# Sparse attention in an audio tower: the choice of places made per half of the batches, inside the work around it

## The reference, cut to what matters

```python
# L = 166: u = int(5 * ln(167)) = 25 places; 38 samples; H = 8 heads of D = 16
K_sample = K[:, :, idx_sample, :]
QK_sample = jnp.einsum('bhld,bhsd->bhls', Q, K_sample) * scale
M = QK_sample.max(axis=-1) - QK_sample.mean(axis=-1)
_, top_idx = jax.lax.top_k(M, u)                     # 25 of 166 places per batch and head
Q_reduce = jnp.take_along_axis(Q, top_idx[..., None], axis=2)
scores = jnp.einsum('bhud,bhld->bhul', Q_reduce, K) * scale
attn = jax.nn.softmax(scores, axis=-1)
V_top = jnp.einsum('bhul,bhld->bhud', attn, V)
out = jnp.broadcast_to(V.mean(axis=2, keepdims=True), (B, H, L, D))
out = out.at[b_idx, h_idx, top_idx].set(V_top)
```

## Time and profile before

| | |
|---|---|
| median of 3 runs | 2203.01 us (2197.26 to 2203.51) |
| profiled execution, its own time | 2204.3 us |
| its span | 2202.5 us |
| sampling | about 544 to 671 us |
| choice | about 671 to 682 us |
| second part of the attention | about 683 to 852 us |

### The profile page before, as it was taken

The page is one execution under the profiler, slowest core; times in us unless marked ns, Lnnn a source line. Parts: engine busy times, 40 slices in busy tenths (PEclk is TensorE's granted clock), DMA queues, the critical chain, the costliest instruction groups (busy, mean ns, idle before and its releaser), DMA issues.

```text
span 2202.5 us, 51244 instructions
## 1 busy us (share of the span) xinstructions
PE 1890.0 (86%) x17246; PEld 1369.7 (62%) x17246; DVE 1698.1 (77%) x4722; ACT 1349.7 (61%) x2009; POOL 1444.1 (66%) x1090
## 2 busy tenths in 40 slices
PE   7989202676996797779999999999999999999998
PEld 5556101454564786557777777777777777777776
DVE  4874701763557875869999999999999999999998
ACT  4113301531442353458888888888888888888886
POOL 2100274005995603338989898898989898988887
PEclk9999656996997899559999999999999999999999
DMA  3512013402332301200000010000100000000000
GB/s 87 165 36 89 17 51 74 79 15 64 113 114 90 102 1 59 79 1 2 1 0 0 1 78 2 0 0 0 78 2 1 0 0 1 2 10 10 10 10 18
DMA packets 66966, 80.63 MB, mean 37 GB/s; under 512 B 33956, under 2 KB 49988, under 8 KB 65156
## 3 DMA queue, kind: packets, MB, share of 16 engines
q1 hardware_dynamic: 64132, 73.22, 10.8%
q0 software_dynamic: 2688, 5.44, 0.8%
HBM read 42.97 MB, written 28.21 MB: 32 GB/s over the span
## 4 chain that ended last, share of the span: by engine, by line
PE 55%; DVE 3%; issue 1%; POOL 0%; ACT 0%; ACTq 0%; DVEq 0%; POOLq 0%
PE bank L2190 28%; PE bank L2173 26%; DVE m_work L2063 1%; DVE m_best L2060 0%; DVE m_work L2054 0%; DVE m_ut L792 0%; PE bank L2142 0%; DVE m_best L2053 0%; DVE m_ex L2065 0%; ACT m_h L2004 0%; DVE h L2101 0%; POOL m_h L1949 0%; DVE m_red L2066 0%; PE bank L784 0%; DVE m_row L2046 0%
## 5 line engine op out<-in xcount | busy, mean ns | idle before, releaser
L2190 PEld LDWEIGHTS bank<-weights,m_h 128*128 128x128 f16 x10752 | 639.2, 98 | 190.0 <-DVE hc L2092 91.9
L1949 POOL TENSOR_TENSOR m_h<-m_hidden,m_h 128x896 f16<-128x896 f32 x384 | 725.4, 1889 | 31.9
L2092 DVE SCALAR_TENSOR_TENSOR hc<-bank,m_shares,hc 128x128 f32<-128x128 f32 x2688 | 727.0, 342 | 4.1 <-PE bank L2190 4.1
L2190 PE MATMUL bank<-weights,m_h 128*128 128x128 f16 x10752 | 724.2, 219 | 2.4 <-POOL m_h L1949 2.4
L2079 DVE TENSOR_TENSOR m_h<-bank,m_h 128x896 f16<-128x896 f32 x384 | 419.2, 1092 | 108.9 <-ACT m_h L2004 108.9
L2001 ACT ACTIVATE m_hidden<-bank,m_b 128x896 f32<-128x896 f32 x384 | 386.7, 1007 | 184.2 <-PE bank L2173 184.2
L1947 POOL TENSOR_SCALAR m_h<-m_hidden 128x896 f16<-128x896 f32 x384 | 359.8, 937 | 111.4 <-ACT m_hidden L2001 87.4
L2173 PE MATMUL bank<-m_u_first,weights 128*128 128x448 f16 (+1 forms) x1536 | 417.6, 354 | 6.9 <-DVE h L2101 5.5
L2173 PE MATMUL bank<-m_u_second,weights 128*128 128x448 f16 (+1 forms) x1536 | 417.3, 353 | 0.0
L1998 ACT ACTIVATE bank<-bank,m_b 128x896 f32<-128x896 f32 x384 | 377.3, 982 | 0.4 <-PE bank L2173 0.4
L2004 ACT ACTIVATE m_h<-bank 128x896 f16<-128x896 f32 x384 | 348.7, 908 | 0.0
(11 more groups left out here) (322 smaller groups left out, 2217.9 us busy)
## 6 DMA issues: line engine op xcount, KB each, us to landing
ew_raw<-e_w_dram SPq DMA_DIRECT2D x32, 512.0 KB, 4.4
expert_factors<-ew_made SPq DMA_DIRECT2D x24, 512.0 KB, 3.0
weights<-expert_factors SPq DMA_DIRECT2D x12, 1024.0 KB, 8.1
expert_slots<-lru_zeros SPq DMA_DIRECT2D x1, 7296.0 KB, 28.6
lru_wst<-w_dram SPq DMA_DIRECT2D x16, 256.0 KB, 2.7
weights<-w_dram SPq DMA_DIRECT2D x1, 4096.0 KB, 12.5
xs<-x_dram SPq DMA_DIRECT2D x4, 996.0 KB, 11.9
out_dram<-h SPq DMA_DIRECT2D x5, 448.0 KB, 2.5
```

The costliest lines, as they stand in the source:

```text
L1949: g.tensor_tensor(h1[:, x, 1], hidden[:, x], h1[:, x, 0], ALU.subtract).then_inc(second_of[1], 1)
L2092: last = v.scalar_tensor_tensor(acc[:, m * TW:(m + 1) * TW], y[q][:, (n - start) * TW:(n - start + 1) * TW], shares[:, m, e:e + 1], acc[:, ...
L2190: last = t.matmul(y[q][:, (n - start) * TW:(n - start + 1) * TW], factors[:, m, n * TW:(n + 1) * TW], k.weights[:, grp % 2, 2 + m, at], st ...
```

## The change

The choice becomes a class `Choice` that works on one group g (16 batches) at a time, with its own buffers.

- Group 0 is chosen within the sampling. TensorE turns its measures in chunk 9, between the two sample products. VectorE copies them in chunk 9, does one round (greatest 8, mark) in each of the chunks 9 to 12 after the second measure, and numbers (compare, scan, product, cast) after the last measure of chunk 13. In chunk 14 TensorE waits for the counts between the two sample products and turns them; VectorE copies them.
- Group 1 is turned at the sampling's end. VectorE copies it at the start of the second part, does a round after each of the batches 0 to 3, and numbers after batch 4. TensorE turns the counts ahead of batch 12, VectorE copies them after batch 12.
- GpSimd's small tables move from the second part into the sampling, ahead of `expand`. The waits for them in the second part go.
- VectorE's and TensorE's chunks 8 to 15 and VectorE's batches 0 to 15 are written out; the rest stays in loops.

```diff
+class Choice:
+    def pe_measures(self, pe, g, m_all, cols):
+        for q in range(2):
+            last = self.nc.tensor.transpose(self.k.bank[:, 6, cols + q * HALF:cols + (q + 1) * HALF],
+                                            m_all[:, q, g * 128:(g + 1) * 128], self.k.ident[0:HALF, 0:HALF])
+        last.then_inc(self.measures, 1)
+    def dve_take(self, dve, g, cols):
+        v = self.nc.vector
+        dve.wait_ge(self.measures, g + 1)
+        v.memset(self.cand[:, L:], SENT).then_inc(self.step, 1)
+        self.n += 1
+        self.link(dve, v.tensor_copy(self.cand[:, 0:L], self.k.bank[:, 6, cols:cols + L]))
+    def dve_round(self, dve, last_round=False):
+        v = self.nc.vector
+        self.link(dve, v.max(self.best[:], self.cand[:]))
+        if last_round:
+            self.link(dve, v.memset(self.best[:, NU % 8:8], SENT))
+        self.link(dve, v.match_replace(self.cand[:], self.best[:], self.cand[:], MARK))
+    def dve_number(self, dve, g):
+        v = self.nc.vector
+        if g:
+            dve.wait_ge(self.turned, g)
+        self.link(dve, v.tensor_scalar(self.chosen[:], self.cand[:, 0:L], CUT, None, ALU.is_le))
+        self.link(dve, v.tensor_tensor_scan(self.count[:], self.k.ones[:, 0:1].broadcast_to([128, L]), self.chosen[:], 0.0,
+                                            ALU.mult, ALU.add))
+        v.tensor_tensor(self.count[:], self.count[:], self.chosen[:], ALU.mult).then_inc(self.counted, 1)
+        dve.wait_ge(self.counted, g + 1)
+        v.tensor_copy(self.rank[:, g], self.count[:]).then_inc(self.kept, 1)
+    def pe_counts(self, pe, g, cols):
+        pe.wait_ge(self.counted, g + 1)
+        for half in range(2):
+            last = self.nc.tensor.transpose(...)
+        last.then_inc(self.turned, 1)
+    def dve_keep(self, dve, g, cols):
+        dve.wait_ge(self.turned, g + 1)
+        self.nc.vector.tensor_copy(self.rank_t[:, :, g * 128:(g + 1) * 128], ...).then_inc(self.kept, 1)
...
+            SPLIT, CHOICE_COLS = NC // 2, 128
+            TAKE, COUNT = SPLIT + 1, NC - 2
...
+                    if isinstance(c, int) and c == TAKE:
+                        choice.dve_take(dve, 0, CHOICE_COLS)
+                    if isinstance(c, int) and c == COUNT:
+                        choice.dve_keep(dve, 0, CHOICE_COLS)
...
+                        if isinstance(c, int) and TAKE <= c <= TAKE + NU // 8 and q == 1:
+                            choice.dve_round(dve, c - TAKE == NU // 8)
+                        if isinstance(c, int) and c == COUNT - 1 and q == 3:
+                            choice.dve_number(dve, 0)
...
                     samples(c, j, 0)
+                    if isinstance(c, int) and c == TAKE:
+                        choice.pe_measures(pe, 0, m_all, CHOICE_COLS)
+                    if isinstance(c, int) and c == TAKE + 1:
+                        pe.wait_ge(choice.step, 2)
+                    if isinstance(c, int) and c == COUNT:
+                        choice.pe_counts(pe, 0, CHOICE_COLS)
+                    if isinstance(c, int) and c == COUNT + 1:
+                        pe.wait_ge(choice.kept, 2)
                     samples(c, j, 1)
...
-            batches(dve, step)
+            choice.dve_take(dve, 1, 0)
+            for b in range(B // 2):
+                step(b, b)
+                if b <= NU // 8:
+                    choice.dve_round(dve, b == NU // 8)
+                if b == NU // 8 + 1:
+                    choice.dve_number(dve, 1)
+                if b == COUNT_AT:
+                    choice.dve_keep(dve, 1, 0)
...
+            choice.pe_counts(pe, 1, 0)
+            pe.wait_ge(choice.kept, 3)
             one_pass(passes - 1, 0, last=True)
```

More of the change, by code:

```diff
@@ L1114, in sparse_attention @@
         hmu = sb("hmu", [128, NH])
-        rank_t = sb("rank_t", [HALF, 2, 2 * 128])
-        rank = sb("rank", [128, 2, L], BF16)
+        choice = Choice(nc, k, ctx)
+        uline = sb("uline", [HALF, NU])
+        urow = sb("urow", [128, 5])
+        hmt = sb("hmt", [GR, 2, NH, DH])
         expand = sb("expand", [128, 16, 2, GR], BF16)
@@ L1193, in _ @@
                         k.expert_weights.pool_pieces(pool, first + c - 1, first + c)
+                g.iota(uline[:], [[1, NU]], base=1, channel_multiplier=0, allow_small_or_imprecise_dtypes=True)
+                g.iota(urow[:, 0:1], [[0, 1]], base=0, channel_multiplier=1,
+                       allow_small_or_imprecise_dtypes=True).then_inc(made, 1)
+                g.memset(hmt[:], 1.0).then_inc(made, 1)
                 g.memset(expand[:], 0.0).then_inc(made, 1)
-                pool.wait_ge(made, 2)
+                pool.wait_ge(made, 4)
+                for q in range(2):
+                    g.affine_select(out=hmt[:, q], in_=hmt[:, q], compare_op=ALU.is_ge, fill=0.0, base=NU * HG * q,
+                                    pattern=[[-NU, NH], [0, DH]], channel_multiplier=1).then_inc(made, 1)
+                pool.wait_ge(made, 6)
+                for q in range(2):
+                    g.affine_select(out=hmt[:, q], in_=hmt[:, q], compare_op=ALU.is_ge, fill=0.0, base=NU - 1 - NU * HG * q,
+                                    pattern=[[NU, NH], [0, DH]], channel_multiplier=-1)
                 g.affine_select(out=expand[:].rearrange("p b g (h u) -> p (b g h) u", h=HG),
@@ L1277, in _ @@
                 link(v.tensor_scalar(hmu[:], k.hm[:], DH ** -0.5, None, ALU.mult))
[L1278 to L1310, removed]
+                for c in range(2):
+                    work(c, c)
+                with dve.Fori(1, SPLIT // 2) as i:
+                    for j in range(2):
+                        work(2 * i + j, j)
+                for c in range(SPLIT, NC):
+                    work(c, c % 2)
             @block.tensor
@@ L1375, in _, with attend @@
                     token_major(0, 0, q)
-                pe.wait_ge(step, 10)
-                chunks(pe, work)
+                pe.wait_ge(step, 9)
+                for c in range(2):
+                    work(c, c)
+                with pe.Fori(1, SPLIT // 2) as i:
+                    for j in range(2):
+                        work(2 * i + j, j)
+                for c in range(SPLIT, NC):
+                    work(c, c % 2)
                 pe.wait_ge(u_summed, NC)
                 pe.wait_ge(q_copied, NC)
-                t.matmul(k.bank[:, 2, 0:B], w_qk[:, 1], u_sum[:], start=True, stop=True)
+                t.matmul(k.bank[:, 2, 0:B], w_qk[:, 1], u_sum[:], start=True, stop=True).then_inc(step_pe, 1)
                 pe.wait_ge(measured, NT)
[L1382 to L1396, removed]
+                choice.pe_measures(pe, 1, m_all, 0)
+        attend(nc, k, q_all, kt_all, v_all, v_mean, w_o, hmu, choice, expand, uline, urow, hmt)
+def attend(nc, k, q_all, kt_all, v_all, v_mean, w_o, hmu, choice, expand, uline, urow, hmt):
     with ExitStack() as ctx:
@@ L1421, in attend @@
         ot = sb("ot", [128, 2, L])
-        made = sem("made")
         prep = sem("prep")
@@ L1461, in _ @@
         def _(pool):
[L1462 to L1474, removed]
             k.expert_weights.pool_pieces(pool, *PIECES_ATTEND)
@@ L1600, in step @@
                 residual(b - 3, x - 3)
-            batches(dve, step)
+            choice.dve_take(dve, 1, 0)
[7 more added lines that the diff above has]
+                    choice.dve_keep(dve, 1, 0)
+            with dve.Fori(B // 2 // U, B // U) as i:
+                for x in range(U):
+                    step(U * i + x, x)
             for b in range(B, B + 3):
```

35 lines of the change are left out of this document (26 added, 9 removed).

## The result

The kernel after takes 2195.82 us (median of 15 runs, 2194.06 to 2200.26); the kernel before, run beside it, takes 2200.21 us (15 runs, 2197.26 to 2204.0). The ratio is 0.998, its 95% interval 0.9973 to 0.9986: 4.4 us or 0.2% less, which is within the 0.3% that I had called no change. I had forecast 2202.0 us, −1.0 against before.

What follows compares the result with a forecast made beforehand. TensorE (86% busy) was taken to bound the sampling, GpSimd's instruction ends to pace the second part's start. Terms -10.4 + 0.5 + 2.8 + 1.7 + 4.2 + 0.2 = -1.0 us gave 2202.0 against the median 2203.0; range 2195 to 2208.

Steps and rivals of the forecast that it cites:

- the clock term: Sampling, behind the chunk 14 wait: TensorE loses the full clock and works at half speed, +1.7 us (0 to 3.4).
- The gap: Between the sampling's last measure and the second part: 11.1 us shrink to 0.75, so -10.4 us.
- Rounds of the first half: Sampling, chunks 9 to 12: each round of some 0.8 us hides in VectorE's waits, cost 0.
- Transposes: Sampling: both pairs for the first half count on TensorE, which has no slack there, +0.5 us.
- wait in chunk 14: Sampling: TensorE stands for the first half's counts between two sample products, +2.8 us (2.0 to 3.6).
- Rounds of the second half: Second part, batches 0 to 3: rounds fit the 1.2 us slack before the held L1546, cost 0; bound +4.2 us.
- Rival B: Sampling and second part: MAX8 and MATCH_REPLACE8 each wait for a GpSimd end too, sum +16.6, 2219.6 us; chance 0.05.
- Numbering the second half: Second part, after batch 4: four held instructions take four GpSimd ends, a whole piece, +4.2 us (0 to 6.5).
- The moved tables: Start of the second part: the first one-hot starts earlier, gain counted at 0, up to 1.5 us if kept.
- Transposes and copy at batch 12: Second part: +0.2 us for TensorE, with the copy before a one-hot hidden.
- D: Sampling and second part: one of the two parts of A comes true, -2.7 or -5.2, 2200.3 or 2197.8 us; chance 0.28.
- A: Sampling and second part: the clock holds and the numbering is hidden, -7.4 with unrolled code, 2195.6 us; chance 0.20.

Runs made afterwards that it cites:

- before_again: The kernel before, unchanged, profiled in another execution; its second part took 165.0 us, against 169.1 in the first profile.
- after_again: The kernel after, unchanged, run again beside the experiments; ratio 0.9974 to the kernel before.
- number_at_10: The kernel after with the second half numbered after batch 10 instead of batch 4; median 3.3 us below after_again.
- rounds_doubled: The kernel after with each round done once more into spare buffers; median 5.8 us over after_again.
- tables_only: The kernel before with only the small tables moved into the sampling; ratio's interval 0.9974 to 1.0007, second part 165.2 us.

## Why the prediction came out as it did

The sign, and "within 0.3%", were right; the time was 6.2 us too high. Of these, 2.8 us are the base (2203.0 was the median of three runs, 2200.2 that of fifteen), and 3.4 us the sum, −1.0 instead of −4.4. Against before_again, whose second part has no clock fall behind the pieces, the stages of after give +2.5 in the sampling, −10.4 in the gap and +3.9 in the second part: −4.0. The other 0.4 us lie in stages that the change does not touch (start +1.5, rest −2.0) and in the measurement. Of the 3.4 us, then, 1.7 are the clock term, 0.9 the wait, and about 0.5 each the second part and the untouched stages. Step by step:

- *The gap, −10.4:* 11.1 to 0.7 us, −10.4. Right.
- *Rounds of the first half, 0:* right. Beside the numbering's wait TensorE stands nowhere longer in the sampling, MAX8 is 330 ns, and it took a second round per chunk to cost 1.5 us.
- *Transposes +0.5 and wait in chunk 14 +2.8:* right in kind, too large. The wait was 1.93 us, just under the lower bound of 2.0. Compare, scan and product of a half took 1.23 us (662.34 to 663.57), as estimated at 1.2; but TensorE reached the place later, at 661.70, and VectorE's last measure, which ended at 662.42, then was only 0.7 us away, not 1.6. Why it came there later no run separates. The fill of `expand` did meet the compare, as the bound had it, but by 0.1 us here and 0.4 at most. Chunks 2 to 15 grew by 2.4 us for 3.3 forecast: 1.9 the wait, and 0.4 to 0.5 for both pairs of transposes.
- *The clock behind that wait, +1.7: this step failed.* I wrote that "a stop of 2.8 us is longer than this", that is than the idle time after which the earlier trace rows show the fall, and put a full 1.7 in the sum. The stop was shorter, and in after and after_again the clock held at 1.00. Where it fell (number_at_10, rounds_doubled) it cost 1.7 us. The size was right, though by its own row the rise came at 553.84, 3.6 us after 550.20 and not 3.4; the event was taken as certain, and it came in two of four profiles, one of them behind a shorter stop than in after. What decides it no run shows. This is half of the 3.4 us.
- *Rounds of the second half, 0:* right. The first four maxima of after come 7.3, 14.9, 21.5 and 28.1 us behind the start, those before 8.4, 14.9, 21.4 and 28.0. Rival B, 2219.6 us, is excluded by the rows of MAX8 and MATCH_REPLACE8. The bound of +4.2 from missed ends was not reached, but rounds_doubled shows it was real: one more round per batch and the ends are missed.
- *Numbering the second half, +4.2:* right. Nine maxima instead of ten, scan and product over 1 us; +3.9 against before_again, and 3.1 of it came back when the numbering was moved behind GpSimd's end. The rest lies where the numbering now stands: 5.2 us between two maxima instead of 4.3. The rule cited from the Trainium skill (SBUF — State Buffer, Who interferes with whom) agrees for all six kinds: the two-input scan and product, the compare and the cast were held beside a GpSimd that reads SBUF, the compare of the first half too (up to 0.65 us for 0.24 alone), MAX8 and MATCH_REPLACE8 were not.
- *The moved tables, 0:* right. The first one-hot is earlier and the next hold takes it back; tables_only shows it alone.
- *Transposes and copy at batch 12, +0.2, and the unrolled code, 0 to −0.5:* no run separates them. Together they leave next to nothing: from the eleventh maximum to the last it is 86.0 us in after and 86.2 in before_again.

Of the cases, what came true is that half of D in which the clock holds and the numbering is held, put at −2.7. The number of A, 2195.6, fits the measured time, but its mechanism is wrong: the numbering was not hidden. The two agree by luck, because the base had moved by 2.8 us.

One thing was to be seen before the run. The mean of 4.23 us per batch in the earlier trace rows contains one interval of 6.8 us, and 5.8 us lie between the two groups of maxima; the others are 4.1. A window from 750 to 770 shows the fall. It would have told me that an execution at 2204.3 carries some 4 us that belong to no step of the ledger. I took its distance of 1.3 us to the median of three for all the noise there was.

## What to carry to other kernels

When a VectorE instruction with two SBUF inputs, or a compare or cast, is put into a stretch where GpSimd works without a break, count it by GpSimd instruction ends and not by its own duration; four short instructions cost 3.9 us of the stage here, and 3.1 came back by moving them behind GpSimd's last piece, at the price of one line. Work moved from a serial place into the slack of another stage should be asked for as late as its consumer allows: the same counts asked for one chunk later were worth 1.6 us of the sampling. And before a sum is made from one profile, look for clock falls in its stages, at their start too, and treat a clock fall behind a pause near 2 us as a chance and not as a cost.

## What the runs showed of the hardware

- The same pause does not always cost the clock: behind 1.93 and 1.96 us it held, behind 2.24 and 1.83 it fell to 1.2 GHz, with nearly the same instructions ahead. The fall cost 1.7 us in both.
- The attention starts at the low clock, and full clock came 8.8 to 11.2 us after its start in the ten profiles. The first two chunks, which no version changes, took 28.1 to 28.4 us in the four profiles where it came by 9.8 us, and 28.4 to 28.9 in the six where it came after 11.0 to 11.2.
- A compare of 166 columns on VectorE, 0.24 us alone, took 0.33 to 0.65 us beside GpSimd's fill of `expand` and each time ended 0.10 us behind the fill's end.
- Between two executions of one kernel a fall of the clock at the end of the GpSimd-paced stretch (mean 0.74 against 1.00 from 750 to 770 us) moved the stage by 4.1 us, nearly as much as the whole change.
- VectorE and GpSimd in alternation can run in orders of different length: 6.54 us per piece in the other profiles, 6.9 in rounds_doubled after its additional rounds, where three of GpSimd's four instructions too were some 0.1 us longer.
- With six idle matmuls per batch the mean granted clock was 0.93 over 78 us, 0.80 without them in the neighbour's profile, and no batch came later.
